# A decoder layer on one core: stores and loads of the self-attention heads reshaped, and the self-attention's side work put on other steps and partly on GpSimd

## The reference, cut to what matters

```python
x = layernorm(x + self_attention(x))         # 32 heads of 16, causal, ALiBi bias, biases on qkv and out
x = layernorm(x + cross_attention(x, ctx))   # 32 query heads of 128, 8 key/value heads, rotary, mask
x = layernorm(x + ffn(x))                    # relu^2 up/down of 1024, a latent path scaled by the
                                             # sum of the two largest of 8 gate logits, own layernorm
```

## Time and profile before

| | us |
|---|---|
| median of 3 runs | 1013.44 |
| the profiled execution | 1012.73 |
| its span, first to last instruction | 1010.9 |
| TensorE busy | 925.9 |
| VectorE busy | 688.1 |
| ScalarE busy | 501.2 |
| GpSimd busy | 484.2 |
| mean granted clock of TensorE | 0.960 of full speed |

### The profile page before, as it was taken

The page is one execution under the profiler, slowest core; times in us unless marked ns, Lnnn a source line. Parts: engine busy times, 40 slices in busy tenths (PEclk is TensorE's granted clock), DMA queues, the critical chain, the costliest instruction groups (busy, mean ns, idle before and its releaser), DMA issues.

```text
span 1010.9 us, 15709 instructions
## 1 busy us (share of the span) xinstructions
PE 925.9 (92%) x4812; PEld 785.1 (78%) x4812; DVE 688.1 (68%) x2195; ACT 501.2 (50%) x1565; POOL 484.2 (48%) x414
## 2 busy tenths in 40 slices
PE   7976999999999877999999999999999986799996
PEld 6855888888888656888888888888888875677885
DVE  5454687776877446777777777777777765565646
ACT  4234777776767115455455454554554553350220
POOL 4542662133212356666666666666666654245101
PEclk9997899998999778999999999999999997999998
DMA  7574985464373540113131121303113111110001
GB/s 251 190 231 99 247 188 126 137 140 131 94 177 106 182 151 21 42 33 115 42 115 32 53 104 33 125 32 124 34 32 126 32 43 54 62 32 21 22 1 42
DMA packets 69395, 96.65 MB, mean 96 GB/s; under 512 B 6208, under 2 KB 43328, under 8 KB 68288
## 3 DMA queue, kind: packets, MB, share of 16 engines
q1 hardware_dynamic: 69312, 95.64, 31.6%
HBM read 68.33 MB, written 27.26 MB: 95 GB/s over the span
## 4 chain that ended last, share of the span: by engine, by line
PE 74%; DVE 8%; issue 6%; ACT 5%; POOL 4%; DMA 2%; SPq 0%; POOLq 0%; DVEq 0%; ACTq 0%
PE banks L34 59%; PE banks L1039 4%; PE banks L1019 3%; PE banks L748 2%; ACT B_prob L650 2%; PE banks L740 1%; PE banks L1040 1%; PE banks L739 1%; DMA heads_k<-heads_k_d 1%; DVE B_prob L796 1%; POOL x L1553 1%; DVE B_pT L817 1%; PE banks L121 1%; PE banks L721 1%; ACT C_prob L986 1%
## 5 line engine op out<-in xcount | busy, mean ns | idle before, releaser
L34 PE MATMUL banks<-C_wo,C_o 128*128 128x512 f32 x768 | 190.2, 396 | 1.0 <-DVE C_o L1131 1.0
L34 PE MATMUL banks<-xT,C_w 128*128 128x512 f32 x768 | 188.3, 395 | 0.0
L34 PEld LDWEIGHTS banks<-xT,C_w 128*128 128x128 f32 x768 | 146.5, 191 | 30.6
L34 PEld LDWEIGHTS banks<-C_wo,C_o 128*128 128x128 f32 x768 | 139.4, 188 | 28.8 <-issue 1.2
L967 ACT ACTIVATE C_q<-C_t 128x512 fp32r<-128x512 f32 x64 | 40.5, 632 | 184.7 <-POOL C_t L1144 184.7
L650 ACT ACTIVATE B_prob<-B_prob,B_top 128x128 f32<-128x128 f32 x256 | 99.3, 391 | 30.5 <-DVE B_top L796 30.5
L1152 POOL TENSOR_TENSOR C_q<-C_t,C_q 128x512 fp32r<-128x512 f32 x64 | 82.7, 1292 | 47.6 <-ACT C_q L967 47.6
L986 ACT ACTIVATE C_prob<-C_prob,C_top 128x128 f32<-128x128 f32 x256 | 99.0, 391 | 0.0
L1144 POOL TENSOR_TENSOR C_t<-C_t,C_t 128x512 f32<-128x512 f32 x64 | 83.2, 1300 | 17.9 <-DVE C_t L1084 17.6
L1039 PE MATMUL banks<-C_kv,C_q 128*128 128x256 f32 x256 | 68.8, 346 | 5.7 <-issue 2.1
L166 POOL TENSOR_TENSOR C_w<-stage,C_w 128x512 fp32r<-128x512 f32 x32 | 41.3, 1292 | 66.5 <-ACT C_w L161 66.5
(11 more groups left out here) (154 smaller groups left out, 2150.3 us busy)
## 6 DMA issues: line engine op xcount, KB each, us to landing
C_kv<-cross_kv_d SPq DMA_DIRECT2D x8, 2048.0 KB, 8.7
cross_kv_d<-B_k_out SPq DMA_DIRECT2D x16, 512.0 KB, 3.1
cross_kv_d<-B_v_out SPq DMA_DIRECT2D x16, 512.0 KB, 4.2
stage<-wq_dram SPq DMA_DIRECT2D x32, 256.0 KB, 2.7
stage<-wo_dram SPq DMA_DIRECT2D x32, 256.0 KB, 2.8
heads_q_d<-cT SPq DMA_DIRECT2D x16, 256.0 KB
heads_k_d<-cT SPq DMA_DIRECT2D x16, 256.0 KB
heads_q<-heads_q_d SPq DMA_DIRECT2D x32, 128.0 KB, 3.8
```

Source lines behind the costliest of these rows:

```text
L34: mm = eng.matmul(out, stationary[i], moving[j], start=first and n == 0, stop=last and n == len(PASSES) - 1)
```

## The change

- `SelfHeads.store`: the tensors in HBM have another layout, and a tile is stored with one DMA of 128 runs of 4 KB instead of two DMAs of 128 runs of 2 KB.
- `SelfHeads.load`: 12 DMAs of 64 KB for each half sequence of heads instead of 8 of 64 and 128 KB, with the same bytes.
- The first sequence's heads are loaded behind the stores of tiles 10 and 12 (`HEADS`) instead of behind all stores and context pieces.
- All 8 value tiles run in stage A; `LATE` and `OFF` are gone, and B's projections begin in step 0, keys and values in turn, keys in bank 6 and values in bank 7.
- In B, a sequence is closed later and its parts stand on other steps: lag 8 and 12 for the two half outputs, 14 transposes, 15 split, 16 and 17 the output product in two halves, 18 residual and statistics, 19 normalising, 20 transposes, 21 splits, with steps of their own for the last two sequences. The drain has 7 steps instead of 12.
- The scaling of the output (L813) and the normalising (L113) go from VectorE to GpSimd, and `normalise` calls `root` itself; the same in D.
- The first query tiles of C are made two to four steps earlier, the scores of C's step 0 are issued in B's step 69, and `exponentials` of step 0 stand before the first `tile_hi`.
- In D: both small products in step 60 with a bank each, and the weight splits of a step ahead of the cross-attention's ScalarE work.
- Some buffers move in SBUF.

```diff
@@ class Rows
     def normalise(self, eng, b):
 
+        self.root(eng, b)
         eng.wait_ge(self.s_rstd, b + 1)
@@ class SelfHeads
+        where = (self.q_d if m < C else self.k_d)[4 * (m % C):4 * (m % C) + 4, :, :, half, :, :]
+        eng.dma_start(where.rearrange("j s d t n -> (j s d) (t n)"), tile.rearrange("p t n -> p (t n)").bitcast(F32))\
+           .then_inc(self.s_store[i % self.RING], 16)
...
+            for term, (qt, kt) in enumerate(((0, 0), (1, 0), (0, 1))):
+                rows = slice((3 * s + term) * DH, (3 * s + term + 1) * DH)
+                for dst, src, t in ((self.q[i][rows, :, :], self.q_d, qt), (self.k[i][rows, :, cols], self.k_d, kt)):
+                    eng.dma_start(dst.bitcast(F32), src[pairs, s, :, b // 4, t, tok].rearrange("j d n -> d j n"))\
+                       .then_inc(self.s_load[i], 16)
@@ class ProjectSelf, sync
             heads.store(eng, i, m, h, self.tiles[i % heads.RING])
-            if i >= self.QK // 2 and i % 2 == 1:
-                self.load_piece(eng, self.CONTEXT + (i - self.QK // 2) // 2)
+            if i in self.HEADS:
+                heads.wait_stored(eng, self.QK // 2)
+                heads.load(eng, 0, self.HEADS.index(i))
+            if i >= self.QK - C:
+                self.load_piece(eng, self.CONTEXT + i - self.QK + C)
         for n in range(self.CONTEXT + C, len(self.pieces)):
             self.load_piece(eng, n)
-        heads.wait_stored(eng, self.QK // 2)
-        for j in range(2):
-            heads.load(eng, 0, j)
@@ class AttendSelf
+    PIECES = (("k", 0, -1), ("v", 0, 0), ("v", 1, 0), ("v", 2, 1), ("v", 3, 1), ("o", 0, 3), ("o", 1, 4), ("k", 1, 6),
...
+    NEXT_SPLIT = {60: 0, 61: 1, 62: 2, 65: 3, 66: 4, 67: 5, 68: 6, 69: 7}
+    QUERY = {64: 0, 65: 1, 66: 2, 67: 3}
+    ROTATE = {65: 0, 66: 1, 67: 2, 68: 3}
...
+    def closing(self, n, lag, ends):
+
+        if n in ends:
+            return B - len(ends) + ends.index(n)
+        b, rest = divmod(n - lag, NG)
+        return b if rest == 0 and 0 <= b < B - 2 else None
+
+    def half_of(self, n, half):
+
+        return self.closing(n, 8 + 4 * half, ((56, 64), (60, 67))[half])
@@ AttendSelf.gpsimd
+        for half in range(2):
+            b = self.half_of(n, half)
+            if b is not None:
+                done = 2 * b + half + 1
+                eng.wait_ge(self.s_oadd, done)
+                eng.wait_ge(self.s_rden, done)
+                o = self.o[:, 16 * half:16 * half + 16, :]
+                eng.tensor_tensor(o, o, self.rden[:, 16 * half:16 * half + 16].unsqueeze(2).broadcast_to([P, 16, DH]),
+                                  ALU.mult).then_inc(self.s_o, 1)
...
-        b = self.normal(n, 0)
+        b = self.closing(n, 19, (65, 69))
         if b is not None:
-            self.rows.root(eng, b)
+            self.rows.normalise(eng, b)
@@ AttendSelf.tensor
-        b = self.closing(n, 5)
+        b = self.closing(n, 14, (62, 67))
...
-        b = self.normal(n, 2)
+        b = self.closing(n, 20, (66, 69))
         if b is not None:
+            if b == B - 1:
+                self.cross.scores(eng, 0)
             eng.wait_ge(self.s_z, b + 1)
             self.rows.transpose(eng, b)
+        for lag, chunks in ((16, (0, 1)), (17, (2, 3))):
+            b = self.closing(n, lag, (64, 68))
+            if b is not None:
+                self.close(eng, b, chunks)
+        if n < 2 * len(self.FILL):
+            self.project(eng, n // 2, n % 2)
@@ class FeedForward
-    LAT = (60, 61)
+    LAT = 60
...
     def turn(self, eng, b):
 
         if b == 0:
-            eng.wait_ge(self.before.s_sin, self.before.TILES)
+            eng.wait_ge(self.s_tlo, self.L)
...
     def vector_ahead(self, eng, n):
 
-        if self.NORMAL <= n < self.NORMAL + B:
-            self.rows.normalise(eng, n - self.NORMAL)
...
     def gpsimd_between(self, eng, n):
 
+        if self.NORMAL <= n < self.NORMAL + B:
+            self.rows.normalise(eng, n - self.NORMAL)
         for i in self.SPLIT.get(n, ()):
             self.piece_lo(eng, i)
-        if self.STATS <= n < self.STATS + B:
-            self.rows.root(eng, n - self.STATS)
```

More of the change, by code:

```diff
@@ L174 @@
     TILES = 4 * C
-    PARTS = 8
+    PARTS = 12
     PAIRS = HS // 4
@@ L344, in scalar @@
             self.piece_hi(eng, n)
-        for i in range(self.BEFORE):
+        for i in range(len(self.order)):
             self.scalar_tile(eng, i)
@@ L373, in tensor @@
                 self.chunk(eng, i, c)
-        for i in range(len(self.acc), self.BEFORE):
+        for i in range(len(self.acc), len(self.order)):
             self.tensor_tile(eng, i)
@@ L643, in scalar @@
             eng.activation(self.pT[0][:, n % 2, :], self.tp, ACT.Copy).then_inc(self.s_phi, 1)
+        b = self.closing(n, 21, (66, 70))
+        if b is not None:
+            self.rows.hi(eng, b)
+        for half in range(2):
+            b = self.half_of(n, half)
+            if b is not None:
+                eng.wait_ge(self.s_pv, NG * b + 4 * half + 4)
+                wait(eng, self.s_ot, b)
+                eng.activation(self.o[:, 16 * half:16 * half + 16, :], self.values_of(half)[:, :, 1, :],
+                               ACT.Copy).then_inc(self.s_olow, 1)
         if self.live(n):
@@ L753, in tensor @@
             wait(eng, self.s_z, b)
-            wait(eng, self.rows.s_lo, b - 1)
-            if b == 0:
-                eng.wait_ge(self.before.s_val, len(self.before.order))
+            wait(eng, self.rows.s_lo, b)
             for c in range(C):
@@ L799, in vector @@
             last.then_inc(self.s_top, 1)
-        if G in (0, 4) and self.live(n, 1):
-            half = 1 - G // 4
-            eng.wait_ge(self.s_exp, n)
-            eng.reciprocal(self.rden[:, 16 * half:16 * half + 16], self.total[:, 16 * half:16 * half + 16]).then_inc(self.s_rden, 1)
-        for half in range(2):
-            b = self.closing(n, 4 * half)
-            if b is not None:
-                done = 2 * b + half + 1
-                o = self.o[:, 16 * half:16 * half + 16, :]
-                eng.wait_ge(self.s_olow, done)
-                eng.tensor_tensor(o, self.values_of(half)[:, :, 0, :], o, ALU.add).then_inc(self.s_oadd, 1)
-                eng.wait_ge(self.s_oadd, done)
-                eng.wait_ge(self.s_rden, done)
-                eng.tensor_tensor(o, o, self.rden[:, 16 * half:16 * half + 16].unsqueeze(2).broadcast_to([P, 16, DH]),
-                                  ALU.mult).then_inc(self.s_o, 1)
         if self.live(n, self.LT):
@@ L818, in vector @@
                               ALU.subtract).then_inc(self.s_plo, 1)
-        b = self.closing(n, 6)
+        b = self.closing(n, 21, (67, 70))
+        if b is not None:
+            self.rows.lo(eng, b)
+        if G in (0, 4) and self.live(n, 1):
+            half = 1 - G // 4
+            eng.wait_ge(self.s_exp, n)
+            wait(eng, self.s_o, n // 4 - 2)
+            eng.reciprocal(self.rden[:, 16 * half:16 * half + 16], self.total[:, 16 * half:16 * half + 16]).then_inc(self.s_rden, 1)
+        for half in range(2):
+            b = self.half_of(n, half)
+            if b is not None:
+                o = self.o[:, 16 * half:16 * half + 16, :]
+                eng.wait_ge(self.s_olow, 2 * b + half + 1)
+                eng.tensor_tensor(o, self.values_of(half)[:, :, 0, :], o, ALU.add).then_inc(self.s_oadd, 1)
+        b = self.closing(n, 15, (63, 67))
         if b is not None:
@@ L1197, in __init__ @@
         self.wlat = [pair("lat0", 140), pair("lat1", 136)]
-        self.hT = [pair(f"hT{t}", 72 + 4 * t if t < 8 else 48 + 4 * (t - 8)) for t in range(self.MT)]
+        self.hT = [pair(f"hT{t}", 72 + 4 * t if t < 8 else (132, 52)[t - 8]) for t in range(self.MT)]
         self.pos, self.sq = pool("pos", 120, [P, 2, D]), pool("sq", 124, [P, 2, D])
```

303 lines of the change are left out of this document (136 added, 167 removed).

## The result

The changed kernel takes 979.1 us (median of 4 runs, 978.3 to 979.7) against 1013.6 (4 runs, 1011.6 to 1014.9): a ratio of 0.966, 95% interval 0.964 to 0.968. The forecast was 975, with 955 to 997 as its range. The profiled execution has a span of 977.4 us against 1010.9, 33.5 less.

The account below looks back on a forecast made before the run. The prediction took TensorE's holes at four places, some followed by a lower clock, to bound the kernel. Its sum was 1012.7 - 4.5 - 12.5 - 9 - 12 = 974.7 us, given as 975, range 955 to 997.

Parts of the forecast that it names:

- A to step 8: Stage A to B's step 8: wait for heads goes, value tiles become late; gain 4.5 us, ends 0 and 8.
- Steps 8 to 63: B's main part: holes shrink as scaling and normalising leave VectorE; gain 12.5 us, ends 3 and 18.
- the 29 that I named as a sign of being wrong: B's sequences still at 29 us would show the forecast wrong.
- the 0.7 us of a late key projection: B, step residue 7 modulo 8: VectorE's 2.1 us of split and second rotation delay the next key projection about 0.7 us.
- (b): ScalarE, or the engines' coupling, holds B's step; steps 8 to 63 gain nothing, 987 us; chance 0.12.
- a stretch at the lower clock: Before the change, B's steps 8 to 63: 20.6 us called holes, 2.6 us a sequence and a lower-clock stretch.
- B's end to C's step 3: From scores 63 to C's step 3: 75.1 us before, 66 forecast; gain 9 us, ends 0 and 18.
- The sign that I named: Between B and C, TensorE's longest wait stands ahead of the last output transposes, released by GpSimd; 6 us.
- the walk: Queue-by-queue estimate from B's end: C's step 3 at 62 us, plus 4 for the lower clock, 66.
- C to D: Step 60 into D: VectorE's waits for the root go with the normalising; gain 12 us, ends 4 and 17.
- (a): GpSimd becomes the bound at the boundaries; gains of 9 and 12 us vanish, 996 us; chance 0.13.
- (c): Heads' loads land too late, TensorE waits in 14 groups; above 1013 us; chance 0.05 with anything else slowing.

Follow-up runs that it names:

- e12: Changed kernel with both output scalings of each sequence (16 instructions) back on VectorE, directly behind their sums: 977.7 us.
- e5: Changed kernel with B's normalising back on VectorE, root on GpSimd; ahead of the second rotation in six regular sequences, behind it in the last two: 980.6 us.
- e6: Changed kernel with normalising between C and D back on VectorE behind the statistics, root still on GpSimd ahead of the weight splits: 979.5 us.
- e1: Changed kernel with four context pieces issued ahead of the heads' loads and the second group of heads' loads behind all stores: 972.6 us.
- e7: Changed kernel with the 4 KB stores and 12-part loads of queries and keys undone, at their new queue places: 985.1 us.
- e8: Changed kernel with TensorE's transposes of normalised x behind the half projection in six regular sequences: 979.8 us.
- e3: Changed kernel with ScalarE taking the transposed output's high part ahead of the step's four exponentials: 972.3 us.
- e4: Changed kernel with the last half of B's last sequence added up and scaled in step 66 instead of 67: 976.3 us.
- e2: Changed kernel with normalising in B back on VectorE behind the second rotation of its step, root on GpSimd: 990.1 us.
- e10: e9 plus VectorE's second rotation ahead of the minima in every eighth step (residue 3): 979.7 us.
- e11: e10 and e8 together, so rotation early and transposes of x behind the projection: 980.9 us.
- e9: Changed kernel with the edits of e1, e3 and e4 together: 964.8 us.

## Why the prediction came out right, and where it did not

The total was right to 4 us. The places were right; the reason given for two of the four gains, work taken off VectorE, was not borne out (e12, e5 and e6); and part of the nearness is luck: errors cancel in A, and a gain that was not forecast stands in D. Term by term:

- *A to step 8: 4.5 forecast, 5.1 measured.* The path was right (scores wait for the last value tile, 3.2 us each; no wait for heads), the shift of the tiles was not. I let them come 1.5 us earlier with 4 later as an end; scores 0 came at 86.9 (85.8 to 88.1 in eight traces). e1 shows the price of SP's issues, 5.5 us, and e7 that the stores' and loads' new form, which I costed at nothing, is worth 6 us here. I had looked at TensorE alone, which showed no hole; ScalarE's six waits for stores stood in the trace of before. Step 8 followed after 25.5 us instead of 28, and that made the sum come out: luck.
- *Steps 8 to 63: 12.5 forecast, 8.5 measured.* Plain sequences are 28.8 to 29.1 us, outside my 27.5 to 28.5 and close to the 29 that I named as a sign of being wrong. I put the 0.7 us of a late key projection at the steps whose number leaves 7 modulo 8. In the trace the output product stands ahead of that projection and covers it; TensorE waits behind the second rotation of the steps that leave 3, to which I had given 1.4 us against 1.3 free (e5 and e8: waits of 0.72 and 0.70 us). What I left out is the hole ahead of the output product: I counted only VectorE's work behind the low part, and the output's high part stood behind four exponentials on ScalarE. e3 measures it at 0.85 us a sequence, 5.2 in these steps: more than the 4 us that are missing. "ScalarE" was my rival (b) as a load; it was ScalarE's order. Off VectorE, the scaling gained nothing (e12) and the normalising 0.4 us a sequence (e5).
- *What the 8.5 us are, then.* The two traces answer it in part. TensorE has the same matmuls between these steps (1225 and 1226), 14.6 us idle before and 7.8 after. Before, a sequence has two holes of about 1.1 us, 13 in all. One is ahead of the transposes of the probabilities, where VectorE has the sum and the scaling of the output in front of their low part; the other is ahead of a value projection, whose bank the second rotation still reads. First two rows of VectorE, then the low part, then TensorE's wait, and last a wait of the second kind:

```profile
162.65 0.36 DVE L810 TENSOR_TENSOR B_o<-banks,B_o 128x256 f32<-128x256 f32 x1
163.05 0.42 DVE L813 TENSOR_TENSOR B_o<-B_o,B_rden 128x256 f32<-128x256 f32 x1
163.39 0.68 DVE L817 TENSOR_TENSOR B_pT<-banks,B_pT 128x512 fp32r<-128x512 f32 x1
164.22 0.63 PE L748 MATMUL banks<-ident,B_prob 128*128 128x128 f32 x4 [1.13 <-DVE B_pT L817]
240.18 2.26 PE L34 MATMUL banks<-B_wv,cT 128*128 128x512 f32 x6 [1.11 <-DVE B_t L846]
```

  In the changed kernel the low part comes first and the sum behind it, and values have a bank of their own:

```profile
271.41 0.69 DVE L822 TENSOR_TENSOR B_pT<-banks,B_pT 128x512 fp32r<-128x512 f32 x1
272.17 0.36 DVE L837 TENSOR_TENSOR B_o<-banks,B_o 128x256 f32<-128x256 f32 x1
```

  Both kinds of hole are gone there, and in e12 too, where the scaling is on VectorE behind the sum; two holes of 0.6 us a sequence have taken their place. So it is order and banks again, as the traces read; no run undid either alone. And 3.2 of the 8.5 us are one fall of the clock in the trace of before, behind the row at 240.18: that sequence took 32.85 us, its neighbours 29.65. The prediction has it as "a stretch at the lower clock".
- *B's end to C's step 3: 9 forecast, 5.7 measured.* The sign that I named is there, the longest wait ahead of L786 and released by GpSimd, 6.19 us against my 6. But the walk ended 3.4 us early (66 against 69.4), and its reading of the wait was wrong in one link: it is GpSimd's queue, but not because the scaling stands in it. With the scaling on VectorE the wait stays at 5.90 (e12); what counts is GpSimd's query sums, which hold ScalarE ahead of the low copy (e4), and the normalising at the head of that queue: with it off GpSimd the wait is 3.1 us in e2 and e5, of which 1.6 reach C's step 3 in e5 and 0.1 in e2. Where the walk lost the rest is open.
- *C to D: 12 forecast, 12.2 measured.* No wait of VectorE for a root is left, the first turn waits 4.02 us for the small products' low parts as forecast (about 4), and the five steps take 8.2, 9.9 (with that wait), 7.6, 5.9 and 5.6 us: 6 to 7 forecast, and none lies in it. e6 shows that taking the normalising off VectorE is not needed. That leaves the other part of my reason, the root ahead of the splits, beside the small products in one step and the earlier splits; which of them gave how much was not run.
- *D: nothing forecast, 2.0 measured*, not followed up. In the traces of e4 and e10, whose D is the changed kernel's, the same stretch took 135.1 us and not 133.5, so most of the 2.0 can be the difference of two executions.
- *C's steps: unchanged*, 7.52 us each. The clock's mean is 0.975, above 0.96.

The rivals: (a) did not come, though the last closing at B's end does hang on GpSimd. (b) was wrong as stated, for the steps did gain. (c) did not come: loads of a group land 4.0 us after issue (median of 96), none was waited for, and the first ones hurt by their issue and not by their landing. The GpSimd normalising took 2.08 us (my estimate 2.2, VectorE 0.54). The Trainium skill (GPSIMD Engine Reference, Engine selection) has one-input operations there roughly at line rate; this case does not agree.

## What to carry to other kernels

Before moving work to another engine, look at which instruction stands in front of the one that the critical engine waits for: three changes of order in one queue (issues on SP, one copy on ScalarE, one step's closing) gave 14 us, while moving 16 scalings or 8 normalisings from one engine to the other changed nothing that the runs can tell, except where the moved instruction was put badly (e2, 11 us). When a hole's releaser is removed and another ends within 0.2 us of it, nothing is won (e5, e8); to test both at once, see what the reordering itself makes late, for in e10 and e11 that hid the answer, and whether the hole goes with both out of the way stays open. And a hole in a matmul-bound loop has two prices: here one of 0.59 us was worth 0.85 (e3), and behind holes of 1.1 to 1.6 us the clock fell in part of the cases, for 1.6 to 3.2 us more each time.

## What the runs showed of the hardware

- Clock, in the sequences of B: behind the changed kernel's 11 idle times of 0.55 to 0.60 us (steps 8 to 63) the granted clock stayed at 1.00, as in e9's row above (4.31 us with 0.65 idle). It fell behind one of 13 of 1.06 to 1.15 us in the kernel before, behind three of six of 1.33 to 1.37 us in e2, and behind five of six of 1.59 us in e10 and in e11. A fall made the sequence 1.6 us longer in e10, 1.6 to 1.7 in e2 and 3.2 in the kernel before. The same hole at the same place of the loop did both, so its length alone does not decide.
- The same scaling of 128 x 256 took 0.62 us on GpSimd (16 times, 0.621 to 0.632) and 0.42 us on VectorE in e12 whenever GpSimd was idle beside it (12 of 16 times). The other four began while a two-input GpSimd instruction ran and took 0.53 to 0.86 us, and each ended 0.28 us after that instruction's end. The last met GpSimd's subtraction that ran from 333.54 to 334.81. VectorE's rows and GpSimd's in e12:

```profile
272.89 0.42 DVE L831 TENSOR_TENSOR B_o<-B_o,B_rden 128x256 f32<-128x256 f32 x1
...
334.23 0.86 DVE L831 TENSOR_TENSOR B_o<-B_o,B_rden 128x256 f32<-128x256 f32 x1
```

```profile
333.54 1.27 POOL L1164 TENSOR_TENSOR C_q<-C_t,C_q 128x512 fp32r<-128x512 f32 x1 [0.74 <-ACT C_q L971]
```

  In the kernel before the median was 0.81: there ten of the 16 scalings met GpSimd, and in e12, on the same engine but in other steps, four did. By the Trainium skill (SBUF — State Buffer, SBUF: two separate sides) the two engines share a pair of ports of which one instruction takes the whole; the four rows that met GpSimd agree, as VectorE's instruction finished only after GpSimd's had.
- SP needed about 0.43 us for most issues of a 64 KB load and 1.2 us for two 256 KB stores of e7: in a queue that also carries the next stage's first input, these are critical.
